# Sorting graph 2's edges into 344 chunks a half instead of 560, with a loop for the edges past them

## The reference

```python
def _gat_block(x, edge_index, W, att_src, att_dst, bias, ln_scale, ln_bias):   # graph 1: N=6250, H=8, C=32
    h = (x @ W).reshape(N, H, C)
    alpha = leaky_relu(a_src[src] + a_dst[dst], 0.2)
    ex = exp(alpha - segment_max(alpha, dst)[dst])
    attn = ex / (segment_sum(ex, dst)[dst] + 1e-16)
    out = segment_sum(h[src] * attn[:, :, None], dst).reshape(N, H * C) + bias
    ...
def _forward(x, edge_index, ...):                                              # graph 2: edges drawn from 0..8191
    h = (x_flat @ W_gat).reshape(M, 4, 4)
    ...                                                                        # the same attention, 4 heads of 4
    scores = layernorm(agg).reshape(M, 4, 4).mean(1)
    w = softmax(top_k(scores, 2))
    for ei in range(4):
        out += g[ei] * (gelu(x @ W1[ei] + b1[ei]) @ W2[ei] + b2[ei])
x = x + gat(layernorm(x));  x = x + experts(layernorm(x))
```

## Time and profile before

| | |
|---|---|
| median of 3 runs | 2449.53 us (2446.08 to 2450.71) |
| span of the profiled execution | 2444.4 us, mean granted clock of TensorE 0.931 |
| loop 1: first gather to the end of the last one | 115.7 to 1301.9 us |
| middle stretch | to 1485.8 us |
| stage 2 | to 2357.9 us |
| scoring and output | to the end |
| busy share PE / DVE / ACT / POOL | 84% / 78% / 34% / 67% |

### The profile page before, as it was taken

How to read it: one execution, slowest core, us unless ns; L and a number is a source line. 1 busy time by engine, 2 the same in 40 slices (tenths; PEclk the granted TensorE clock), 3 DMA queues, 4 the chain that set the end, 5 groups by cost and what they waited for, 6 DMA issues and landing times.

```text
span 2444.4 us, 38890 instructions
## 1 busy us (share of the span) xinstructions
PE 2062.8 (84%) x10736; PEld 1309.7 (54%) x10820; DVE 1901.8 (78%) x5345; ACT 827.6 (34%) x2023; POOL 1639.1 (67%) x1778
## 2 busy tenths in 40 slices
PE   5767787699999989999967777999999899899816
PEld 3534444455555545555544555665656556555615
DVE  7588998899999999999987983665555555555558
ACT  3431111133333323333313653443434344343313
POOL 1466777777777767777774555777777777777700
PEclk9988998799999989999988887999999999999958
DMA  6344444444444444444446002223322322222259
GB/s 195 107 133 111 127 124 124 123 124 120 122 116 118 122 110 117 116 119 122 116 124 177 3 7 44 78 74 85 74 70 70 85 74 70 67 69 70 61 186 354
DMA packets 159493, 263.20 MB, mean 108 GB/s; under 512 B 42246, under 2 KB 81988, under 8 KB 159268
## 3 DMA queue, kind: packets, MB, share of 16 engines
q0 software_dynamic: 61376, 124.22, 21.6%
q1 hardware_dynamic: 97892, 136.33, 17.4%
HBM read 219.59 MB, written 40.84 MB: 107 GB/s over the span
## 4 chain that ended last, share of the span: by engine, by line
PE 49%; DVE 20%; issue 15%; POOL 9%; DVEq 2%; DMA 2%; ACT 1%; SPq 1%; ACTq 0%; POOLq 0%
PE pb L1344 11%; PE pb L1256 8%; PE pb L1242 8%; PE pb L1227 7%; POOL early L712 3%; PE pb L1360 3%; DVE x_sb L2369 2%; POOL dl L712 2%; PE pb L1228 2%; POOL tab L712 2%; DVE big L1648 2%; PE pb L1219 2%; PE pb L1134 1%; DVE x_sb L2278 1%; DVE Gb L1684 1%
## 5 line engine op out<-in xcount | busy, mean ns | idle before, releaser
L778 POOL DMA_INDIRECT Gb<-table,idx x560 | 595.3, 1063 | 231.7 <-issue 155.4
L1256 PE MATMUL pb<-Gb,early 128*128 128x256 f32 x1568 | 400.5, 400 | 44.1 <-DVE idx L2441 44.0
L1242 PE MATMUL pb<-big,Gb 128*128 128x512 f32 (+1 forms) x832 | 414.6, 614 | 10.2 <-DVE acc L1806 8.8
L2369 DVE TENSOR_SCALAR x_sb<-iota,x_sb 128x610 bf16<-128x610 f16 x1024 | 407.4, 439 | 0.0
L1344 PE MATMUL pb<-Gb,Sall 128*128 128x264 f32 x1120 | 371.0, 429 | 41.2 <-DVE big L1648 41.0
L1256 PEld LDWEIGHTS pb<-Gb,early 128*128 128x128 f32 x1568 | 292.2, 196 | 133.1 <-DVE idx L2441 58.5
L778 POOL DMA_INDIRECT early<-table,idx x272 | 291.2, 1071 | 94.5 <-issue 74.3
L1227 PE MATMUL pb<-x_sb 128*128 128x512 bf16 x940 | 323.5, 380 | 4.6 <-DVE x_sb L2369 3.5
L857 ACT ACTIVATE x_sb<-pb 128x512 f16<-128x512 f32 x256 | 152.9, 597 | 399.6 <-PE pb L1219 399.6
L712 POOL DMA_INDIRECT dl<-table,idx x224 | 219.6, 980 | 86.4 <-issue 82.8
L867 ACT ACTIVATE early<-pb,b1c 128x512 f32<-128x512 f32 (+1 forms) x208 | 137.8, 663 | 398.3 <-PE pb L1242 398.0
(11 more groups left out here) (461 smaller groups left out, 3323.1 us busy)
## 6 DMA issues: line engine op xcount, KB each, us to landing
Sall<-dlT SPq DMA_DIRECT2D x186, 256.0 KB
Y<-idx SPq DMA_DIRECT2D x96, 256.0 KB, 2.0
big<-Y SPq DMA_DIRECT2D x16, 1024.0 KB, 11.4
x_sb<-in_x_dram SPq DMA_DIRECT2D x8, 1536.0 KB, 16.1
Gb<-table,idx POOLq DMA_INDIRECT x560
early<-table,idx POOLq DMA_INDIRECT x480
out_dram<-x_sb SPq DMA_DIRECT2D x24, 256.0 KB
Gb<-in_L_ffn_W_dram SPq DMA_DIRECT2D x8, 512.0 KB, 6.9
```

Source lines behind the costliest of these rows:

```text
L778: g.indirect_dma_start(out=G1[i % 3][:, k, :], out_offset=None, in_=g1.table, in_offset=bass.IndirectOffsetOnAxis(ap=g1.idx[:, c:c + 1], a ...
L1242: t = pe.matmul(pbank[b][:, 0:nt * 128], W1s[:, w, k, f * 128:f * 128 + 128], xT[:, t0:t0 + nt, k * 128:k * 128 + 128], start=k == 0, stop ...
L1256: t = pe.matmul(pbank[b][:, 0:D], hh[:, bi % 2, f, j * 128:j * 128 + 128], W2s[:, w, f, :], start=f == 0, stop=f == 3)
L2369: v.tensor_scalar(Bv[j % NB], iota16[:, 0:HW], winF[:, k:k + 1], bE[:, k:k + 1], ALU.is_equal, ALU.mult).then_inc(v_bv, 1)
```

## The change

Each half now has room for 344 chunks (`HC`), and both together for 656. A one-hot over chunks is 394 wide (344 + 50), and one matmul of 394 columns takes the place of two. The cost of a place step in the list is 320 instead of 400, the total 569,940. Edges that don't fit are marked in a step `left` behind the picks (one tensor_scalar on 128x1024, two operations on 128x512 and two on 128x1024, then a transfer of 256 KB by SP), and a flag says whether there are any. The flag is tested on DVE, PE, ACT and SP ahead of the expert steps that open stage 2, and again where graph 2's maxima are made, if the flag for that is set; behind it is a loop over 1024 columns and 49 tiles. The tail sections are gone. In its core the diff is:

```diff
-HC = 560
+HC = 344
...
-            q.NCH = -(-(-(-q.E // BLK) + T * q.n - 1) // q.W) * q.W
+            q.NCH = -(-(-(-q.E // BLK) + T - 1) // CG) * CG if q.n == 1 else 656
+            wide = q.NCH if q.n == 1 else 1136
...
-        SECT = [41, 42] + list(range(45, NC2 // W2, 3)) + [NC2 // W2]
-        NSEC = len(SECT) - 1
+        ROUNDS = NC2 // W2
...
-        def hot_bank(g):
-
-            return pbank[7 if g < HB // 4 + 2 else 5]
...
-            yield 4000, [("tails",)]
...
+            yield 4000, [("left",)]
...
-                yield 400, ops
+                yield 320, ops
...
+                if i == LEFT_AT + 3:
+                    sp.wait_ge(s_left, 1)
+                    sp.dma_start(left_d, leftD).then_inc(l_left, 16)
             sp.wait_ge(s_idx2, 2)
+            sp.wait_ge(l_left, 16)
...
-            reg, rn = g.alloc_register("g_tail"), g.alloc_register("g_tailn")
-            g.wait_ge(s_tails, NSEC)
-            g.load([reg], flags[0:1, 4:5])
-            g_edges2(g, main2, 0, SECT[0], 0)
-            with g.If_ne(reg, 0):
-                g.wait_ge(main2["v_ad"], DONE2)
-                g_edges2(g, tail2, SECT[0], SECT[1], SECT[0])
-                for n in range(1, NSEC):
-                    g.load([rn], flags[0:1, 4 + n:5 + n])
-                    with g.If_ne(rn, 0):
-                        g_edges2(g, tail2, SECT[n], SECT[n + 1], SECT[0])
-            g.free_register(rn)
-            g.free_register(reg)
...
-                pe.matmul(pbank[5 + 2 * w][:, :], A, Bv[n][:, 0:512], start=j % HB == 0, stop=j % HB == HB - 1)
-                pe.matmul(pbank[6][:, 128 * w:128 * w + HW - 512], A, Bv[n][:, 512:HW], start=j % HB == 0,
-                          stop=j % HB == HB - 1).then_inc(p_pl, 1)
+                pe.wait_ge(a_av, hot_at(j // 4) - 1)
+                pe.matmul(pbank[5 + 2 * w][:, 0:HW], A, Bv[n], start=j % HB == 0, stop=j % HB == HB - 1).then_inc(p_pl, 1)
...
-                p_map_row(pe, g2, s_tm2, 1, (5, 6, 7))
+                p_map_row(pe, g2, s_tm2, 1, (5, 6))
...
+            v.wait_ge(l_left, 16)
             v.memset(x_sb[:, T - 1, :], 0.0).then_inc(s_xz, 1)
...
+            v.wait_ge(s_start2, 1)
+            v_left(v)
             for step in ffn_steps[0:PRE2]:
                 for op in step:
                     v_ffn(v, op)
-            v.wait_ge(s_start2, 1)
-            reg, rn = v.alloc_register("v_tail"), v.alloc_register("v_tailn")
-            v.wait_ge(s_tails, NSEC)
-            v.load([reg], flags[0:1, 4:5])
-            v_edges2(v, main2, 0, SECT[0], 0, True, "b")
-            with v.If_ne(reg, 0):
-                v.wait_ge(main2["v_ad"], DONE2)
-                for n in range(NSEC):
-                    def section():
-                        v_edges2(v, tail2, SECT[n], SECT[n + 1], SECT[0], False, f"z{n}")
-                        v.wait_ge(tail2["v_ad"], (SECT[n + 1] - SECT[0]) * W2)
-                    if n == 0:
-                        section()
-                    else:
-                        v.load([rn], flags[0:1, 4 + n:5 + n])
-                        with v.If_ne(rn, 0):
-                            section()
-            v.free_register(rn)
-            v.free_register(reg)
+            v_edges2(v, main2, 0, ROUNDS, 0, True, "b")
             v.wait_ge(main2["v_ad"], DONE2)
 
 
...
+        def v_left(v):
+            tab8 = g2.tab[:, 0:T * 8].rearrange("p (t w) -> p t w", w=8)
+            reg = v.alloc_register("v_left")
+            v.load([reg], flags[0:1, 4:5])
+            with v.If_ne(reg, 0):
+                v.wait_ge(l_back, 48)
+                with v.Fori(0, J2) as j:
+                    jv = v.snap(j, min_val=0, max_val=J2 - 1)
+                    v_left_column(v, jv)
...
+                v.tensor_scalar(lim[:, 0:1], g2.cum[:, T - 1:T], float(HC), None, ALU.min).then_inc(*c.one())
...
+                v.tensor_scalar(g2.cum[:, 0:T], g2.cum[:, 0:T], lim[:, 0:1], None, ALU.min).then_inc(*c.one())
+                v.wait_ge(*c.now())
+                v.tensor_scalar(flags[0:1, 4:5], stc[0:1, 0:1], lim[0:1, 1:2], None, ALU.is_gt).then_inc(s_tails, 1)
+                v.tensor_scalar(g2.cum[:, T:2 * T], g2.cum[:, T:2 * T], lim[:, 1:2], lim[:, 0:1], ALU.min, ALU.add).then_inc(*c.one())
+                v.tensor_scalar(lim128, lim, 128.0, None, ALU.mult).then_inc(*c.one())
+                v.wait_ge(*c.now())
+                v.wait_ge(s_tails, 1)
...
-            if op[0] == "tails":
-                for n, gi in enumerate(SECT[:-1]):
-                    v.tensor_scalar(flags[0:1, 4 + n:5 + n], g2.cum[0:1, 2 * T - 1:2 * T], float(W2 * gi), None, ALU.is_gt).then_inc(
-                        s_tails, 1)
+                v_map_row(v, g2, s_map2, 2, (5, 6), op[1])
+            if op[0] == "left":
+                v.wait_ge(v_pk, 2 * T)
+                v.tensor_scalar(bF2, bF2, 1.0, None, ALU.min).then_inc(*c.one())
+                v.wait_ge(*c.now())
+                for h in range(2):
+                    o = slice(HB * h, HB * h + HB)
+                    v.scalar_tensor_tensor(left16[:, o], pos2[:, o], lim128[:, h:h + 1], bF2[:, o], ALU.is_ge, ALU.mult).then_inc(*c.one())
+                v.wait_ge(*c.now())
+                v.scalar_tensor_tensor(pos2, left16, 2.0 ** 18, pos2, ALU.mult, ALU.add).then_inc(*c.one())
+                v.scalar_tensor_tensor(leftD, dst2, 1.0, left16, ALU.add, ALU.mult).then_inc(s_left, 1)
...
+                v.memset(g2.idx[:, 0:NC2], 0).then_inc(*c.one())
+                v.memset(g2.dl[:, 0:NC2], 512.0).then_inc(*c.one())
+                v.memset(g2.dl16[:, 0:NC2], 512.0).then_inc(*c.one())
...
-                    v.tensor_copy(dcd[0][:, 0:512], pbank[5 + 2 * w][:, :]).then_inc(*c.one())
-                    v.tensor_copy(dcd[0][:, 512:HC], pbank[6][:, 128 * w:128 * w + HC - 512]).then_inc(*c.one())
-                    once = pbank[6][:, 128 * w + HC - 512:128 * w + HC - 512 + T]
+                    v.tensor_copy(dcd[0], pbank[5 + 2 * w][:, 0:HC]).then_inc(*c.one())
```

286 lines of the change are left out of this document (208 added, 78 removed).

## The result

The changed kernel takes **2412.95 us** (median of 4 runs, 2410.95 to 2415.18) against 2450.12 us for the kernel before: a ratio of 0.9848, 95% interval 0.9835 to 0.9861. The profiled execution's span is 2409.2 us, against 2444.4, with a mean granted clock of 0.930. The forecast was 2421 us and a gain of 28; the gain is 35 to 37.

| stretch | before | after | difference | forecast |
|---|---|---|---|---|
| to the first gather of loop 1 | 115.7 | 117.0 | +1.3 | 0 |
| gathers of groups 0 to 32 | 374.7 | 368.6 | -6.1 | -2 |
| gathers of groups 33 to 96 (places, decode 0) | 733.9 | 709.4 | -24.5 | -17 |
| the rest of loop 1 (decode 1) | 77.6 | 76.3 | -1.3 | -3 |
| middle stretch, to the first gather of stage 2 | 183.8 | 181.7 | -2.1 | -0.8 |

What follows compares the result with a forecast made beforehand. POOL was to pace the place groups, DVE close behind, PE out of the bound. 17 + 3 + 2 + 0.8 + 5.5 = 28 us off 2444.4 gave a span of 2416, so 2421 us; own range 2412 to 2431, full range 2400 to 2440.

Steps and rivals of the forecast that it cites:

- The end of stage 2: Between DVE's last addition and first scoring instruction: the 5.57 us branch over the tail sections goes, -5.5 us.
- The matmul: Place groups on PE: one matmul of 394 columns for a pair, 9.7 us a group, PE out of the bound.
- the rival of a falling clock: Place groups: PE's clock falls to 0.82, PE paces at 11.8 us a group, 2465 us in all; chance 0.05.
- `left`: Step behind the picks: 4.4 us of DVE, once, in group 25, covered by POOL: 0, at most +4.
- The one-hot's price: Place groups on DVE: 216 columns fewer save 45 ns, so 0.31 us for each one-hot.
- the rival of 18 ns: Place groups on DVE: the narrower one-hot saves only 18 ns, 2446 us, no change; chance 0.13.
- The flag: Rival that the flag fires: the loop over 1024 x 49 steps would take 10 ms; chance 0.01.
- DVE's own sum: Place group on DVE: 11.17 us busy, less 5.79, plus 5.58 for 18 one-hots, gives 10.96.
- the floor: Place group on POOL: eight gathers of 1.389 us, 11.11 us, untouched by the edit.
- the rival of shorter gathers: Place groups on POOL: gathers shorten with the one-hots, POOL needs 10.85 us a group, 2403 us in all; chance 0.17.
- Groups 0 to 32: Early groups of loop 1: the picks lie thinner, which takes away the last waits there, -2 us.
- Decode 1: End of loop 1: narrower decode operations give back 8 us for both halves on DVE, -3 counted on the path.

Runs made afterwards that it cites:

- that part alone: Kernel before with the tail sections' code and branches taken out on all engines, nothing else: 2442.64 us, ratio 0.9979.
- slots 2 and 6: Changed kernel with 18 columns in every place group and the third one-hot column fixed at these slots of eight: 2395.9 us, 0.9778 of the kernel before.
- slots 1 and 5: Changed kernel with 18 columns in every place group and the third one-hot column fixed at these slots of eight: 2422.54 us, 0.9887 of the kernel before.
- two steps more: Changed kernel with each place matmul four columns behind its one-hot instead of two: 2394.59 us, 0.977 of the kernel before.
- The last run: Changed kernel with 17 columns a group, third always in slot 2, place matmul four columns behind its one-hot: 2771.23 us, 0.9916 of the kernel before.

## Why the prediction was right, and where it wasn't

**Right in mechanism and size.** *The end of stage 2*: 5.5 us forecast, 5.5 in the trace, 6.0 for that part alone. *The matmul*: PE leaves the bound, and its clock stays at 1.00; the rival of a falling clock didn't come. *`left`*: its five operations measure 0.4 + 2 x 0.75 + 2 x 1.2 = 4.3 us (4.4 forecast), and groups 24 to 32 take 10.83 us with it and 10.81 without. *The one-hot's price*: 45 ns forecast, 56 from start to start, 42 by the mean durations, in which the held ones count; the rival of 18 ns is out. *The flag* stayed zero.

**Right in sum, wrong in the step that gives it.** The prediction said that POOL would pace, at 8 x 1.389 = 11.11 us, with DVE close behind, and that POOL's waits would nearly vanish, to under 8 us. They rose to 30 us in half 1 alone. What paces is DVE, with what its one-hots lose beside gathers and the pause behind its register load. DVE's own sum was nearly right: 10.96 us of work forecast, 10.91 at slots 2 and 6. But its idle time was carried over as 0.2 us a group, and it is 0.10 there and 0.41 at slots 1 and 5. The forecast of 11.17 us a group stands beside 11.13 measured over groups 38 to 96 only because three kinds of group average to it: 10.4 at first, while POOL fills the buffers ahead of DVE, 11.0 at slots 2 and 6, and 11.5 at slots 1 and 5. The step that failed is the floor: a gather's mean of 1.084 us was taken for POOL's own cost, "untouched by the edit". But it was measured beside a DVE that was full. Slots 2 and 6 against 1 and 5, and the one-hots 16 wide (0.985), show that a part of it belongs to what DVE does beside it. The row of the gathers by itself, in the trace of before, carried the warning: the shortest took 940 ns and the median 994. The prediction had the sign of this in the rival of shorter gathers (0.17), with too weak an argument against it, that one-hots take nearly as much of a group as before.

In the traces one-hots and gathers do hold each other up: gathers take 1.152 us at 610 columns and 0.985 at 16, and held one-hots end 83 to 94 ns after a gather's end at 394 columns and 139 to 149 ns after it at 610. The Trainium skill ("SBUF — State Buffer", Who interferes with whom) has it that VectorE's two-port operations and GpSimd exclude each other. The runs agree; they show the delay, not the port.

The Trainium skill's rate of four elements a cycle ("VectorE: DVE Perf Modes", The perf-mode tier table) gave 56 ns for 216 columns; from start to start the median of a one-hot went from 350 to 294 ns, which is just that, and the 45 ns worked out from other rows' scalars were too few.

**Not in the prediction.** It counted 16.3 against 18 columns a group as amounts, and didn't ask which slot the eighteenth falls into. Between the best place and the worst lie 27 us. The place could be read in the order of the changed kernel, and its price, by groups, in the trace of before: 0.14 us for an extra column in slot 2 and 0.49 in slot 6. The register load that makes slot 2 cheap was there too, with the same 0.95 us.

**Terms off in size.** Groups 0 to 32 gave 6.1 us instead of 2, 5 of them in groups 0 to 7, where the steps lie thinner now. Not all of it is the change's: the kernel before without tails, with the old spacing, needs 2 us less there than the kernel before. The row of 128 to 222 us before and after:

```profile
128.00:222.00 94.00, 67.55 (x336) 39.02 (x337) 80.58 (x208) 22.24 (x26) 59.90 (x57) 0.79 0.40 110
```
```profile
128.00:222.00 94.00, 66.21 (x342) 39.92 (x342) 79.27 (x196) 23.16 (x27) 62.86 (x61) 0.84 0.44 117
```

Four gathers more fit into the same time. Decode 1 gave 1.3 us instead of 3; the 8 us that the prediction has for both halves on DVE are 9 to 14 by its own rows (50 operations of 0.45 to 0.74 us, 216 of 560 columns less), so that hardly any of it lay on the path. Stage 2 took 3.1 us more instead of the same: a gather L724 takes 985 ns in the mean of 656, where it was 979. The kernel before without tails has 979 and the same 872 us. Of the nine other kernels on the changed one that were timed at the usual pace with their edges in place, seven have 983 to 985 ns and 874 to 875 us; the other two, with the third column at slots 3 and 7 and at 0 and 4, have 981 and 980 ns and 873 us. What does this was not found.

## What to carry to other kernels

When engines are full together, the mean duration of an operation that another engine can hold up (here a gather on POOL) is no floor; only a run that frees the other engine shows it. A pause that the profile calls "issue" and that comes once in each group is worth following into the engine's sequencer: here a load of registers that takes 0.95 us shows only where the engine has too little queued work to cover it, and an odd step put in front of it was free. A list of costs that spaces steps leaves a remainder, and where the odd step falls can cost as much as the edit earns: sort the groups of the trace by that place before pricing, and fix it. And when an edit to an order gives the gain that was expected of it, check that it moved nothing else; here two steps more shifted the rest, and that was most of the gain.

## What the runs showed of the hardware

**A gather on POOL can hold up a tensor_scalar on DVE, to its own end.** 147 of the changed kernel's 166 one-hots of over 430 ns end 83 to 94 ns after a gather's end. In the slow groups about four are held in each, for 0.49 us in all. Unhindered, 394 columns take 0.294 us from start to start. In the kernel before, with 610 columns, all 105 one-hots of over 450 ns end 139 to 149 ns after a gather's end. That is 56 ns later, just what the 216 further columns take, as if a held one-hot did all its columns behind the gather.

**A load of registers on DVE takes about a microsecond, and work already queued hides it.** Four registers (L1672) take 0.948 us in the median of 98, eight (L1677) 1.828 us in 6. The one-hots queued ahead of it run meanwhile; the next addition starts 0.22 us after the load's end. With two one-hots between, DVE stood 0.31 us in the median slow group, with three it did not.

**A branch over much code costs microseconds, over little code half of one.** DVE's branch over 1598 rows held it up for 5.57 us, and taking the code out gave 6.0 us of the kernel's time; the one over a short body had cost 0.49.

**Gathers of one and the same row are slow.** In the kernel with one-hots 16 wide nearly all indices of graph 2 are zero, so that its gathers fetch the same 128 times. Stage 2 takes 1215.5 us instead of 875.2, with POOL's own time for a gather unchanged (977 ns). The queue's packets take over twice the time for the same bytes; the page's rows of the changed kernel and of this one (packets, MB, share of 16 engines):

```profile
q0 software_dynamic: 61376, 124.22, 22.3%
```
```profile
q0 software_dynamic: 61376, 124.22, 50.7%
```

**The same kernel can be 14% slower on another chip with hardly longer instructions.** The last run showed it (2795.16 us against 2449 to 2451 for the kernel before): gathers of 1.02 us as elsewhere, one-hots of 390 ns in the mean, matmuls 3 to 6% longer, and most of the difference in the time between instructions.
